# Turning the attention output straight out of its PSUM bank, with the residual's sums later on GpSimd

## The reference, cut to what matters

```python
y = einsum('bhqk,bhkd->bhqd', softmax(att), v)            # self
y = y + einsum('bhqk,bhkd->bhqd', softmax(attc), vc)      # cross
y = y.transpose(0, 2, 1, 3).reshape(x.shape[0], T, C)
x = x + (y @ Wp + bp)                                     # projection and residual
```

## Time and profile before

| | us |
|---|---|
| median of 3 runs | 1555.88 |
| lowest, highest | 1555.67, 1558.64 |
| the profiled execution, its own time | 1554.58 |
| its span in the trace | 1552.8 |
| TensorE busy in the span | 1443.6 |
| VectorE busy | 1169.3 |
| ScalarE busy | 900.6 |
| GpSimd busy | 548.4 |

### The profile page before, as it was taken

One profiled execution on the slowest core, in us unless ns is written; L12 is line 12 of the kernel. 1 busy time (PEld: TensorE's weight loads), 2 busy tenths in 40 slices (PEclk: granted clock), 3 DMA queues, 4 the chain that ended last, 5 costly groups with the idle time before them and its releaser, 6 DMA issues. The chain is left out here.

```text
span 1552.8 us, 25660 instructions
## 1 busy us (share of the span) xinstructions
PE 1443.6 (93%) x8558; PEld 694.2 (45%) x8560; DVE 1169.3 (75%) x3215; ACT 900.6 (58%) x1754; POOL 548.4 (35%) x1012
## 2 busy tenths in 40 slices
PE   8899999999999999999999999899989857999997
PEld 4443343444344444433443444344433323676674
DVE  6879888988898898879888988798786177455451
ACT  2067777777777777767767777677667501112111
POOL 4042243341444234432434341443113212453452
PEclk8599999999999999999999999999999967999999
DMA  6875565829383846576475729282800120444443
GB/s 177 115 136 93 95 105 124 102 73 150 103 109 83 159 91 97 103 153 92 89 126 138 95 79 134 95 118 70 133 3 3 42 87 15 126 96 119 126 93 51
DMA packets 82388, 155.22 MB, mean 100 GB/s; under 512 B 13008, under 2 KB 46416, under 8 KB 82256
## 3 DMA queue, kind: packets, MB, share of 16 engines
q1 hardware_dynamic: 74752, 142.43, 48.6%
q0 software_dynamic: 6144, 8.52, 3.3%
q10 hardware_dynamic: 1360, 2.62, 0.5%
HBM read 96.52 MB, written 53.08 MB: 96 GB/s over the span
## 5 line engine op out<-in xcount | busy, mean ns | idle before, releaser
L842 ACT ACTIVATE probs<-bank_ps 128x512 f32<-128x512 f32 (+1 forms) x1408 | 721.6, 580 | 231.6 <-PE bank_ps L633 227.7
L948 DVE TENSOR_REDUCE chunk_max<-bank_ps 128x1 f32<-128x512 f32 x1024 | 651.5, 682 | 88.7 <-PE bank_ps L672 83.7
L633 PE MATMUL bank_ps<-q_stack,k_stack 64*128 64x512 f32 (+3 forms) x1536 | 510.5, 423 | 44.5 <-ACT probs L842 43.2
L672 PE MATMUL bank_ps<-k_stack,q_stack 62*128 62x512 f32 (+3 forms) x1536 | 531.3, 436 | 20.3 <-DVE chunk_max L948 14.6
L672 PEld LDWEIGHTS bank_ps<-k_stack,q_stack 62*128 62x128 f32 x1536 | 251.6, 193 | 377.6 <-DVE chunk_max L948 250.8
L633 PEld LDWEIGHTS bank_ps<-q_stack,k_stack 64*128 64x128 f32 x1536 | 240.0, 189 | 126.9 <-ACT probs L842 124.3
L651 PE MATMUL out_ps<-probs,v_cross 128*32 128x512 f32 x2048 | 276.4, 612 | 0.0
L951 DVE CUSTOM_DVE_ANT_0 masked<-bank_ps,causal 128x128 bf16<-128x128 f32 (+3 forms) x512 | 232.1, 484 | 57.7 <-PE bank_ps L672 55.5
L1147 POOL TENSOR_TENSOR pool_idle<-pool_idle 128x1 f32<-128x1 f32 x292 | 57.1, 196 | 594.3 <-ACT probs L842 365.1
L1480 ACT ACTIVATE h<-h_ps,b1T 128x512 f32<-128x512 f32 x64 | 44.0, 687 | 227.1 <-PE h_ps L1412 195.4
L1412 PE MATMUL h_ps<-ff_yT,w1T 128*128 128x512 f32 x256 | 113.0, 595 | 0.6 <-DVE ff_yT L1493 0.6
(11 more groups left out here) (172 smaller groups left out, 1355.5 us busy)
## 6 DMA issues: line engine op xcount, KB each, us to landing
parts_dram<-parts SPq DMA_DIRECT2D x70, 512.0 KB, 2.7
k_stack<-parts_dram SPq DMA_DIRECT2D x180, 192.0 KB, 14.4
q_stack<-parts_dram SPq DMA_DIRECT2D x180, 128.0 KB, 13.4
w1T<-in_L_ffn_fc1s SPq DMA_DIRECT2D x8, 1024.0 KB, 5.8
w2T<-in_L_ffn_fc2s SPq DMA_DIRECT2D x8, 1024.0 KB, 7.6
z_rows<-z_sb SPq DMA_DIRECT2D x8, 528.0 KB, 13.9
x_sb<-in_x SPq DMA_DIRECT2D x8, 512.0 KB, 3.9
ctxT<-in_ctx SPq DMA_DIRECT2D x8, 512.0 KB, 12.7
```

The lines of the kernel that those rows point to most:

```text
L633: mm = pe.matmul(bank_of(turn)[:, of.at:of.end], k_stack[base:base + SIDE, g, pair, of.keys:of.keys + P], q_stack[base:base + SIDE, g, pai ...
L672: return pe.matmul(bank[:, 0:n], q_stack[base:base + MAX_ROWS, g, pair, qc:qc + P], k_stack[base:base + MAX_ROWS, g, pair, k0:k0 + n], sta ...
L842: nc.scalar.activation(probs[:, buffer(u, i, p), side, columns], bank_of(("score", g, i, p, side))[:, columns], ACT.Exp, scale=SCALE)\
L948: nc.vector.tensor_reduce(dst, bank[:, 0:n], AX.X, ALU.max).then_inc(max_done, 1)
```

## The change

ScalarE's 64 copies `copy_out` go, and with them `u_ready`. VectorE's turn reads `out_ps` itself and writes `u_sb`. The turns leave the table and stand at two fixed iterations, ahead of what the table lists and ahead of the second-to-last maximum: the self turn of the unit before in iteration 2, the cross turn of the same unit in iteration 10. TensorE waits for the turns (`turned`) where it waited for the copies. The divides and turn_backs stay where they were. After the last unit the self turn comes ahead of both divides. On GpSimd the residual's sums go from (0, 6) to (1, 4).

```diff
 OUTPUT_PLAN = {
-    (0, 1): ("turn_cross",), (0, 2): ("divide_cross",), (0, 6): ("turn_self",), (0, 8): ("divide_self",),
...
+    (0, 2): ("divide_cross",), (0, 8): ("divide_self",), (0, 9): ("turn_back",), (1, 1): ("divide_cross",),
+    (1, 3): ("divide_self",), (2, 2): ("divide_cross",), (2, 5): ("divide_self",), (3, 2): ("turn_back",),
+    (3, 5): ("divide_cross",), (3, 8): ("divide_self",),
 }
...
                 if i in (0, CROSS_IT) and (u > 0 or i > 0):
-                    pe.wait_ge(u_ready, 2 * u + (i > 0))
+                    pe.wait_ge(turned, 2 * u + (i > 0))
...
-            def copy_out(b, g, s):
-
-                u = UNITS * b + g
-                act.wait_ge(pv_done, ITS * u + (ITS if s else CROSS_IT))
...
-                nc.scalar.copy(u_sb[:, s, :], out_ps[:]).then_inc(u_ready, 1)
-
...
             def turn_heads(unit, s):
 
-                dve.wait_ge(u_ready, 2 * unit + s + 1)
-                nc.vector.transpose(u_sb[:, s], u_sb[:, s]).then_inc(turned, 1)
+                dve.wait_ge(pv_done, ITS * unit + (ITS if s else CROSS_IT))
+                nc.vector.transpose(u_sb[:, s], out_ps[:]).then_inc(turned, 1)
...
                             if n == ahead_of_pieces(i):
+                                if i == BEHIND and UNITS * b + g > 0:
+                                    turn_heads(UNITS * b + g - 1, 1)
+                                elif i == CROSS_IT + BEHIND:
+                                    turn_heads(UNITS * b + g, 0)
                                 for name in outputs_at(first, g, i):
                                     output(b, g, name)
...
-                        if (g, i) == (0, 6) and not first:
+                        if (g, i) == (1, 4) and not first:
                             residual(b - 1)
```

More of the change, by code:

```diff
@@ L364, in attention @@
         pv_done = sem("pv_done")
-        u_ready = sem("u_ready")
         rden_done = sem("rden_done")
@@ L900, in batch @@
                             add_value_bias(b - (g == 0), int(g == 0))
[L901 to L906, removed]
             def store_parts(piece):
@@ L928, in _ @@
             batch(B - 1, False, True)
-            copy_out(B - 1, UNITS - 1, 1)
             add_value_bias(B - 1, 1)
@@ L1022, in output @@
                     turn_back(b - (g == 0), int(g == 0))
-                elif name.startswith("turn"):
-                    turn_heads(unit, int(name == "turn_self"))
                 else:
@@ L1120, in _ @@
             batch(B - 1, False, True, False)
+            turn_heads(UNITS * B - 1, 1)
             for s in range(2):
-                turn_heads(UNITS * B - 1, s)
                 divide(UNITS * B - 1, s)
```

## The result

The changed kernel takes 1566.39 us (median of 4 runs, 1565.92 to 1566.81), the kernel before 1555.78 beside it (4 runs, 1554.92 to 1558.64): a ratio of 1.0065, with a 95% interval from 1.0047 to 1.0082. So it is 0.65% slower. The forecast was 1563.7 us, with a range from 1549 to 1576.

What follows compares the result with a forecast made beforehand. TensorE, busy 1443.6 of 1552.8 us, was taken as the bound. 1554.6 + 24.4 (turn) - 16.6 (residual) = 1562.4 in the profiled execution, 1.3 us under the median: 1563.7 us, range 1549 to 1576.

Steps and rivals of the forecast that it cites:

- The cross turn in iteration 10: TensorE's values of (g, 8) wait for VectorE's turn at 30 places: 1.08, 0.71 or 0.30 us each, +24.4 us together.
- the hand-over: From the turn's end on VectorE to TensorE's values: 0.05 us for the semaphore.
- its bounds of 0.64 and 0.80: VectorE's fastest and slowest pass over a PSUM bank, bounding the 703 ns turn; -1.9 to +2.9 us over 30 places.
- The estimate of 0.77 us: VectorE's turn out of PSUM by the skill's fixed costs, 65 ns more; would make the turn's term 2 us larger.
- The residual's sums: On GpSimd, moved to (1, 4): VectorE's wait for the sum of the heads goes whole, -16.6 us.
- The copies and the self turn: ScalarE's copies, 37.6 us, bring 0; the self turn in iteration 2 costs 0, or 9 us if its cover were gone.
- The old places: 45 us of VectorE's turns leave eight iterations of each batch: no gain, upper bound 22.2 us.
- the wait was given back: Rival: iterations after 10 return up to 0.6 us of each stall, 18 us, giving 1546; chance 0.10.
- the 0.1 us that the prediction named as a sign against it: The forecast is wrong if iterations after 10 are shorter than before by more than 0.1 us.
- The falls of the clock: Rival: behind the new waits TensorE's clock falls four to nine times more, adding 5 to 21 us, about 1575; chance 0.15.
- the residual's gain: Rival on GpSimd: the residual's gain doesn't come, 1580 us in full, 1572 by half; chance 0.05.
- ScalarE's didn't: Rival: gains on ScalarE's side are real, 9.6 us in the 32 iterations 2, giving 1554; chance 0.10.

Runs made afterwards that it cites:

- experiment 1: The kernel before with only the residual's sums moved from (0, 6) to (1, 4): 1536.20 us, ratio 0.9849 to the kernel before.
- experiment 2: The changed kernel with the residual's sums back at (0, 6), so only the turns are changed: 1576.61 us, ratio 1.0118 to the kernel before.
- experiment 6: The changed kernel with the cross half again copied by ScalarE and turned at its old places, self half straight from PSUM: 1535.01 us, ratio 0.9848 to the kernel before.
- experiment 5: The changed kernel with the cross turn ahead of the second maximum of iteration 10: 1544.20 us, ratio 0.9918 to the kernel before.
- experiment 4: The changed kernel with the cross turn ahead of the fifth maximum of iteration 10: 1603.79 us, ratio 1.0288 to the kernel before.

## Why the prediction was right, step by step

**The cross turn in iteration 10** held in its mechanism and its places: 30 waits, one in every unit up to 29, none in 30 and 31, with the order of the groups as worked out. Its size was 27.5 us instead of 24.4, since each wait is 0.11 or 0.12 us longer than 1.08, 0.71 and 0.30; only g = 0 of the last batch, which the prediction took to be as g = 1, has 0.92 for 1.08, as its iteration takes 3.12 us without a wait and not 2.75. The term that was mis-sized is the hand-over: I had taken 0.05 us from the turn's end to TensorE, and it takes 0.15 (437.24 to 437.39). The remaining 0.01 is the turn itself, 712 ns for 703, well inside its bounds of 0.64 and 0.80. The estimate of 0.77 us by the Trainium skill ("VectorE: DVE Perf Modes", the section on the TRN2 errata) was not borne out: with PSUM as the source this instruction took 9 to 11 ns more, not 65.

**The residual's sums** gave -16.2 us, by the stretches of experiment 1: 1.71, 0.81, 4.15, 4.61 and 4.94 for 1.72, 0.82, 4.16, 4.61 and 5.31. The step rested on reading the undisturbed batch 5 as what batches 2, 3, 4 and 6 would become, and that held; batch 7 was given the 5.45 us of unit 9 and took 5.82, so its part was 0.37 us too large. Counting the falls of the clock behind the waits as part of them held too. What the prediction didn't say is that the step would be worth less, 12.3 us, if only the turn were changed (experiment 2).

**The copies and the self turn** at nothing: experiment 6 has half of the copies and all self turns direct, and up to batch 6 no iteration 2 is shorter or longer by more than 0.02 us. For the other half, the cross copies, experiment 5 shows it: without them iteration 10 takes 3.54 us in g = 0 and 3.13 in g = 2, as with them. TensorE's waits for an exponential were 46.2 us, no less than the 43.2 before, and ScalarE's waits for scores grew by 69.3 us, more than the 37.6 us of copies that went. *The old places* of the turns gave nothing either; those iterations are the same to 0.02 us.

**The rivals.** Next to nothing of the wait was given back: the iteration after each has the length of before, save behind g = 3, where it takes 2.70 us for 2.81 or 2.83 in four batches. That is just beyond the 0.1 us that the prediction named as a sign against it, and worth 0.5 us in all. The falls of the clock came in part. Their number did not grow (5 for 6), but three of the six went with the residual's waits, which experiment 1 confirms with 2 falls, so some two or three came with the turn. Two of the five stand directly behind one of the new waits of 1.13 and 1.28 us, shorter than the 1.49 us behind which the prediction saw none. They cost 1.1 us each, so the total stayed near the forecast. With the turn 0.6 us later, in experiment 4, there are 15. The other two rivals can be read off the rows above: the residual's gain came all but 0.4 us, and ScalarE's didn't.

**The total.** +27.5 - 16.2 + 0.5 (clock) = 11.8, for the +7.8 of the sum: the turn missed by 3.1 us, the residual by 0.4 and the clock by 0.5, all in the same direction, so no error of a term was hidden by another. That the clock's part is so small is luck: it is the balance of falls at different places. The measured medians differ by 10.6 us.

## What to carry to other kernels

Work that moves to another engine costs what comes last behind its place in that engine's order, not its length: the same 0.71 us cost TensorE 1.20, 0.24, 0.39 and 1.80 us at four places of one iteration (ahead of the fourth maximum, the second, the first and the fifth), and nothing where a piece covered it. Before an engine is relieved, look for who waits for it. ScalarE's 37.6 us were worth nothing: in unit 9, iteration 10, TensorE waited 0.24 us for an exponential with the copies (experiment 1) and 0.23 without them (experiment 5). And take a change with two parts apart: this one held a gain of 1.5% (sums that wait for a load, moved behind the work that is wanted soon) under a loss of 2%.

## What the hardware showed that was not expected

- **The hand-over depends on what is handed over.** From the end of a transpose out of PSUM to the values it took 0.14 to 0.15 us in the timelines shown (437.24 to 437.39; 432.27 to 432.42; 449.84 to 449.98). From the end of a maximum to the product that reuses its bank it took 0.06 (431.50 to 431.56). The values stand behind two waits, for the turn and for the mask, that product behind one; whether that makes the difference or the instruction does was not separated.
- **A transpose of 128 x 512 fp32 costs the same from either memory** within 11 ns (711 ns out of PSUM and 700 out of SBUF in one kernel).
- **The granted clock fell more often where TensorE stood idle, whatever it waited for.** Waits once per unit of 1.5 us on average (45.8 us at 30 places) went with 15 falls in the attention, the same lateness with three unused products in it with 3, and waits of 0.85 us on average (25.6 at 30) with 5. Without a wait for the turn there were 2 (experiment 1) and none (experiment 6). Each of these is a count in one profiled execution.
